# A two-layer graph attention kernel: a front built features first, with spread scores, an adding transfer for the keys and reordered early slots

## What is computed

```python
h = x @ W
e = leaky_relu((h @ a_src)[:, None] + (h @ a_dst)[None, :], 0.2)
valid = (adj > 0) & (h.sum(axis=1) != 0)[None, :]
att = softmax(where(valid, e, NEG)); att = where(valid, att, 0)
L = valid.sum(axis=1)
att = where(att >= 1e-4, att, 0) * L[:, None]      # and 0 where the row's top is not over 1e-4
x = layernorm(x + elu(h + att @ h))
s = leaky_relu(x @ ks.T, 0.2)
x = layernorm(x + softmax(where(adj > 0, s, NEG)) @ ks)
```

## Time and profile before

| | us |
|---|---|
| median of 3 runs | 864.79 |
| lowest, highest | 864.57, 865.67 |
| the profiled execution | 863.84 |
| its span in the trace | 862.0 |

### The profile page before, as it was taken

How to read it: one execution, slowest core, us unless ns; L and a number is a source line. 1 busy time by engine, 2 the same in 40 slices (tenths; PEclk the granted TensorE clock), 3 DMA queues, 4 the chain that set the end, 5 groups by cost and what they waited for, 6 DMA issues and landing times.

```text
span 862.0 us, 17646 instructions
## 1 busy us (share of the span) xinstructions
PE 837.0 (97%) x7111; PEld 718.3 (83%) x7111; DVE 787.5 (91%) x993; ACT 766.2 (89%) x747; POOL 234.1 (27%) x450
## 2 busy tenths in 40 slices
PE   7789999999999999999999999999999999999995
PEld 4668888888988888898888888988888898888885
DVE  2998999999999999999999999999999999999745
ACT  4799999999999999999999999999999999999653
POOL 1371123233212232321223233222232321222100
PEclk9799999999999999999999999999999999999998
DMA  9948766667787666678766666886766678620000
GB/s 221 227 88 164 142 106 121 130 132 137 151 153 107 126 127 130 132 147 154 135 112 122 129 133 139 152 152 103 127 124 136 132 149 154 101 42 21 4 2 10
DMA packets 35713, 105.02 MB, mean 122 GB/s; under 512 B 6960, under 2 KB 19376, under 8 KB 27824
## 3 DMA queue, kind: packets, MB, share of 16 engines
q0 software_dynamic: 16608, 65.02, 51.4%
q1 hardware_dynamic: 18592, 38.80, 12.9%
q10 hardware_dynamic: 432, 0.07, 0.1%
HBM read 136.38 MB, written 2.10 MB: 161 GB/s over the span
## 4 chain that ended last, share of the span: by engine, by line
PE 90%; DVE 3%; POOL 2%; DMA 2%; issue 1%; ACT 1%; POOLq 0%; SPq 0%; ACTq 0%; DVEq 0%
PE bank L342 26%; PE work L243 26%; PE bank L366 13%; PE bank L367 7%; PE work L319 6%; PE work L320 6%; PE work L324 6%; DMA mask<-adj 1%; POOL gate L912 1%; DMA att<-x 1%; PE bank L372 1%; DVE att L729 1%; POOL coef L916 1%; DVE mask L616 0%; ACT att L454 0%
## 5 line engine op out<-in xcount | busy, mean ns | idle before, releaser
L243 PE MATMUL work<-ident,att 128*128 128x128 f32 x2080 | 259.5, 276 | 11.4 <-DMA att<-x 5.7
L243 PEld LDWEIGHTS work<-ident,att 128*128 128x128 f32 x2080 | 236.8, 144 | 19.1 <-issue 6.7
L342 PE MATMUL bank<-h_all,att0T 128*128 128x128 f32 x2048 | 244.3, 275 | 0.0
L342 PEld LDWEIGHTS bank<-h_all,att0T 128*128 128x128 f32 x2048 | 236.2, 192 | 0.2 <-ACT att0T L478 0.2
L366 PE MATMUL bank<-k_parts,att1T 128*128 128x257 f16 x1024 | 182.9, 275 | 0.0
L367 PE MATMUL bank<-k_parts,att1T 128*128 128x129 f16 x1024 | 178.0, 219 | 0.0
L500 ACT ACTIVATE att1T<-work 128x1024 f16<-128x1024 f32 x128 | 131.3, 1027 | 39.2 <-PE work L243 39.2
L695 DVE SCALAR_TENSOR_TENSOR att1T<-work,att1T 128x1024 f16<-128x1024 f32 x128 | 152.2, 1210 | 3.6 <-ACT att1T L500 3.6
L645 DVE SCALAR_TENSOR_TENSOR att<-att,cut 128x2048 f32<-128x2048 f32 x64 | 150.0, 2347 | 0.0
L684 DVE CUSTOM_DVE_ANT_0 att<-att,mask 128x2048 f32<-128x2048 f32 x64 | 146.0, 2284 | 2.4 <-ACT att L484 2.4
L484 ACT ACTIVATE att<-work 128x1024 f32<-128x1024 f32 x128 | 127.7, 1026 | 19.5 <-PE work L324 19.5
(11 more groups left out here) (97 smaller groups left out, 675.4 us busy)
## 6 DMA issues: line engine op xcount, KB each, us to landing
mask<-adj POOLq DMA_DIRECT2D x32, 1024.0 KB, 8.6
mask_zero<-zero_cols SPq DMA_DIRECT2D x29, 1024.0 KB, 5.0
mask_zero<-adj POOLq DMA_DIRECT2D x29, 1024.0 KB, 11.7
att<-x SPq DMA_DIRECT2D x4, 512.0 KB, 6.6
x_sb<-x SPq DMA_DIRECT2D x32, 64.0 KB, 2.8
out<-x SPq DMA_DIRECT2D x32, 64.0 KB, 4.9
k_parts<-ks POOLq DMA_DIRECT2D x1, 1024.0 KB, 12.9
w_sb<-W ACTq DMA_DIRECT2D x1, 64.0 KB, 2.8
```

The lines of the kernel that those rows point to most:

```text
L243: mm = pe.transpose(work[:, n % SLOTS, b * P:(b + 1) * P], source(c * PER + b), ident[:, :])
L342: mm = pe.matmul(acc0, att0T[:, k * P:(k + 1) * P], h_all[:, k, :], start=(k == 0), stop=(k == BLOCKS - 1))
```

## The change

Six things are changed.

1. **Features first, one matrix of 131 columns.** `w_sb` holds W and, beside it, all three columns of W a (source, destination, sum). `make_h` runs right behind the transposes of x, in the fills' order `FIRST`, and gives every block's h and its three numbers, which `keep_parts` puts into `node_parts`. A fourth place (`sums`, two banks) joins the three of `work`. DVE takes chunks 1 and 3 of x and the first two fills of h; ACT takes the rest.
2. **Destination scores and zero columns spread by transposes.** `turn_d` transposes one column of `node_parts`, read 128 times over, so that all rows hold the same 128 scores. `test_zero` (DVE, 8 columns) makes the zero test per node, and `turn_zero` spreads it the same way in bf16, with a bf16 identity. `make_d`, `find_sign`, `zero_quarter` and the widened columns are gone.
3. **Adjacency tile 0 in two halves**, issued when chunks 0 and 2 of x are in; the fp16 keys are issued right behind tile 1 and no longer wait for it, and `k_first` (fp32 keys, SP) waits for tile 1 and no longer for tile 0.
4. **The keys' low parts by an adding transfer.** `negate_k` writes minus the high parts into `k_parts`, and POOL issues a load that adds the fp32 keys to them. `k_parts` is one column wider, so that its rows are of even length. `keep_k_low` is gone.
5. **The first tile.** One exponential over 4096 columns, four cuts of 1024, four separate semaphore counts for the transposes, and the coefficient of tile 0 on DVE.
6. **The first four slots have an order of their own** (`first_slot`, `early_slots` on PE, `early_slot` on ACT and DVE), and slot 3 takes the exponentials of tile 4 and its cut later.

```diff
@@ tensor
+            def make_h(r):
+                blocks = range(r * H_PER, min((r + 1) * H_PER, BLOCKS))
+                c = blocks[-1] // PER
+                pe.wait_ge(w_ready, 1)
+                pe.wait_ge(xT_ready[c % 2], c // 2 + 1)
...
+            def turn_d(c):
+                wait_parts(pe, (c + 1) * PER - 1)
+                turn(place_of("d", c), c, lambda b: node_parts[:, b, 1:2].to_broadcast([P, P])).then_inc(d_turned, 1)
+
+            def turn_zero(k):
+                pe.wait_ge(zero_tested, k + 1)
+                pe.wait_ge(ident16_ready, 1)
+                for b in range(PER):
+                    mm = pe.transpose(zero_place(k)[:, b * P:(b + 1) * P],
+                                      zero_block[:, k * PER + b:k * PER + b + 1].to_broadcast([P, P]), ident16[:, :])
+                mm.then_inc(zero_turned, 1)
...
+            def early_slots():
...
+                sum1(0, 0)
+                turn1(0, 3, True)
+                sum1(0, 1)
+                turn_q(1)
+                sum1(0, 2)
+                for c in range(CHUNKS):
+                    score(1, c)
...
+                sum0(2, 1)
+                sum1(0, 3)
+                turn1(1, 0, True)
+                sum0(2, 2)
+                sum0(2, 3)
@@ vector
-            def keep_k_low():
+            def negate_k():
+
                 dve.wait_ge(k_high, 16)
-                dve.wait_ge(kall_in, 16)
-                nc.vector.tensor_tensor(k_parts[:, :, 0:D], k_first, k_parts[:, :, D:2 * D], ALU.subtract).then_inc(k_low, 1)
+                nc.vector.tensor_scalar(k_parts[:, :, 0:D], k_parts[:, :, D:2 * D], -1.0, None,
+                                        ALU.mult).then_inc(k_negated, 1)
...
+            def test_zero(k):
+                blocks = slice(k * PER, (k + 1) * PER)
+                wait_parts(dve, (k + 1) * PER - 1)
+                nc.vector.tensor_scalar(zero_block[:, blocks], node_parts[:, blocks, 2], 0.0, -NO_EDGE, ALU.is_equal,
+                                        ALU.mult).then_inc(zero_tested, 1)
@@ gpsimd
-            pool.wait_ge(xall_in[1], 16)
-            load_adj(0)
+
+            pool.wait_ge(xall_in[0], 16)
+            nc.gpsimd.dma_start(mask[0][:, half(0)], adj_rows[0][:, half(0)]).then_inc(first_adj_in[0], 16)
+            pool.wait_ge(xall_in[2], 16)
+            nc.gpsimd.dma_start(mask[0][:, half(1)], adj_rows[0][:, half(1)]).then_inc(first_adj_in[1], 16)
             pool.wait_ge(xall_in[3], 16)
             load_adj(1)
 
-            pool.wait_ge(adj_in[1], 16)
             pool.wait_ge(k_one_ready, 1)
             nc.gpsimd.dma_start(k_parts[:, :, D:2 * D], ks.rearrange("(b p) d -> p b d", p=P)).then_inc(k_high, 16)
             load_adj(2)
-            coefficient(0)
-            add_adj(EARLY)
+            add_adj(3)
+            pool.wait_ge(k_negated, 1)
+            nc.gpsimd.dma_start(k_parts[:, :, 0:D], ks.rearrange("(b p) d -> p b d", p=P),
+                                accum_op=ALU.add).then_inc(k_low, 16)
```

More of the change, by code:

```diff
@@ L262, in make_h @@
[L262 to L273 removed]
+                turn(place_of("x", c), c, lambda b: x_all[:, b, :]).then_inc(x_turned, 1)
@@ L386, in first_slot @@
                     score(0, c)
+            def early_slots():
+                score(0, 3)
+                turn0(1, 0)
+                turn0(1, 1)
+                turn0(1, 2)
+                sum0(1, 0)
+                turn0(1, 3)
+                sum0(1, 1)
+                sum0(1, 2)
+                turn1(0, 0, True)
+                turn1(0, 1, True)
+                sum0(1, 3)
+                turn1(0, 2, True)
+                sum1(0, 0)
[5 more added lines that the diff above has]
+                    score(1, c)
+                turn0(2, 0)
+                turn0(2, 1)
+                turn0(2, 2)
+                sum0(2, 0)
+                turn0(2, 3)
+                sum0(2, 1)
[3 more added lines that the diff above has]
+                sum0(2, 3)
+                turn1(1, 1, True)
+                turn1(1, 2, True)
+                turn1(1, 3, True)
+                sum1(1, 0)
+                turn_q(2)
+                sum1(1, 1)
+                for c in range(3):
+                    score(2, c)
             def slot(t):
@@ L422, in _ @@
             first_slot()
-            for t in range(1, TILES):
+            early_slots()
+            for t in range(EARLY_SLOTS + 1, TILES):
                 slot(t)
@@ new lines, in early_slot @@
+            def early_slot(t):
+                u = t - 1
+                copy0(t, 0)
+                copy0(t, 1)
+                raise0(t + 1, t % 2)
+                copy0(t, 2)
+                if t == 1:
+                    copy0(t, 3)
+                raise1(u, 0)
+                raise1(u, 1)
+                if t > 1:
+                    copy0(t, 3)
+                copy1(u, 0)
+                if t > 1:
+                    raise0(t + 1, 1)
+                elu_exp(t)
+                copy1(u, 1)
+                copy1(u, 2)
+                copy1(u, 3)
+                q_high_part(t)
+                bend0(t + 2)
+                for c in range(CHUNKS):
+                    bend1(t, c)
@@ L606, in _ @@
             first_slot()
-            for t in range(1, TILES):
+            for t in range(1, EARLY_SLOTS + 1):
+                early_slot(t)
+            for t in range(EARLY_SLOTS + 1, TILES):
                 slot(t)
@@ L813, in first_slot, with early_slot @@
                 cut(1, 1)
-                zero_mask(3)
+            def early_slot(t):
+                u, w = t - 1, t - 2
+                mask1(u, 0)
+                mask1(u, 1)
+                offset1(u)
+                zero_mask(t + 2)
+                mask0(t + 2)
+                if w >= 0:
+                    finish1(w)
+                low_part1(u, 0)
+                residual0(t)
+                elu(t)
+                low_part1(u, 1)
+                normalise0(t)
+                low_part1(u, 2)
+                threshold0(t + 1)
+                q_low_part(t)
+                low_part1(u, 3)
+                if t + 1 >= EARLY:
+                    build_mask(t + 1)
+                cut(t + 1, 0)
+                cut(t + 1, 1)
             def slot(t):
@@ L828, in slot @@
                     mask0(t + 2)
+                if t == EARLY_SLOTS + 1:
+                    threshold0(t + 1)
+                    cut(t + 1, 0)
                 residual0(t)
@@ L860, in _ @@
             first_slot()
-            for t in range(1, TILES):
+            for t in range(1, EARLY_SLOTS + 1):
+                early_slot(t)
+            zero_mask(EARLY_SLOTS + 3)
+            for t in range(EARLY_SLOTS + 1, TILES):
                 slot(t)
@@ L866, in _ @@
         def _(pool):
-            nc.gpsimd.memset(ones[:, :], 1.0).then_inc(consts_ready, 1)
             nc.gpsimd.memset(ident[:, :], 0.0).then_inc(consts_zeroed, 1)
```

423 lines of the change are left out of this document (239 added, 184 removed).

## The result

| | before | changed |
|---|---|---|
| median of 16 runs each, us | 864.76 | 863.20 |
| lowest, highest | 863.60, 866.10 | 862.65, 863.94 |
| profiled execution, its span | 863.84, 862.0 | 863.02, 861.2 |

The changed kernel is faster by 1.56 us: ratio 0.9984, 95% interval 0.9978 to 0.9990, thus 0.9 to 1.9 us. That is just inside the 0.2% that counts as no change.

What follows compares the result with a forecast made beforehand. The prediction took slot 3's start, set by DVE's list with PE's further lead given back, as the bound: 3.0 us earlier, less 0.6 and 0.2, makes 2.2 us less, 862.6 us. Its range was 859.4 to 866.5.

Steps and rivals of the forecast that it cites:

- it is wrong if slot 3 does not start 3 us earlier on DVE: Its own test: DVE's first layer-1 mask of slot 3 at 114.7 against 117.69, 3.0 us earlier.
- the sum 3.0 - 0.6 - 0.2: DVE's earlier slot 3, less the threshold wait in slot 3, less the collision with POOL's load: 2.2 us gained.
- no slot becomes shorter: Slots 3 to 31: left as they are apart from small edits in slot 3, still 24.9 us each.
- PE's start: Front: small loads in at 6.6 us, half pace to 10.4, then h fills and x chunks at full pace to 16.3.
- The late rise of the clock: Rival, PE in the front: clock stays at its lower level throughout, ledger 12 us later, 876.8; chance 0.03.
- slow transposes: Rival, PE's fills from 16.3 to 25.4: broadcast transposes take double, -1.0 to -6.2 us, 867.5 in one case; chance 0.09.
- slow negation: Rival, DVE in the first slot: negation takes 4.4 us instead of 1.2, total -0.8, 865.6; chance 0.08.
- late tile 1: Rival, DVE's mask in the front: adjacency tile 1 lands at 23, not about 20.8, total -1.0, 865.8; chance 0.12.
- The collision with POOL's adding load of tile 3: Near 40.3 us its issue meets DVE's mask of tile 2: full price 0.9, or nothing; 0.2 taken.
- The adding key load: POOL in the first slot: issue of some 1.72 us after the negation, x1 of tile 0 at 55.9, transfer hidden.
- PE's lead is given back: Early slots: PE 5.4 us earlier, DVE only 3.0; slot 3 gives back the 2.4 between them.
- The 0.6 us for the threshold in slot 3: Slot 3: threshold of tile 4 waits 0.6 us for an exponential that ACT now does later.

Runs made afterwards that it cites:

- e3: Changed kernel with POOL issuing the adding key load behind the deviation of tile 0, not ahead of it: 860.02 us, ratio 0.9947 to the kernel before.
- e4: Changed kernel with the order of slots 1 to 3 on PE, ACT and DVE put back to the old one: 862.99 us, ratio 0.9980.
- e9: e3 with the order of slots 1 to 3 on PE, ACT and DVE put back to the old one: 859.12 us, ratio 0.9946.
- e1: Kernel before with only the rows of k_parts made 258 columns long, not 257: 863.93 us, ratio 0.9990.
- e2: Changed kernel with the rows of k_parts back at 257 columns: 864.19 us, ratio 0.9998 to the kernel before.
- e6: e3 with PE's first work reordered, x chunk 0 turned ahead of the weights and the wait for the small loads: 858.59 us, ratio 0.9943.
- e10: Changed kernel with 35 identity transposes that compute nothing in PE's wait ahead of x1 of tile 0: 861.78 us, ratio 0.9968.
- e11: e6 with 13 identity transposes that compute nothing in PE's gap ahead of x1 of tile 0: 859.23 us, ratio 0.9936.
- e12: e7 with 13 identity transposes in PE's gap ahead of x1 of tile 0 and 18 at the very start: 856.88 us, ratio 0.9908.
- e7: e6 with DVE building the mask of adjacency tile 1 one step later: 859.73 us, ratio 0.9944.
- e8: Changed kernel with the keys' low parts made by DVE's subtraction again and no adding load: 864.19 us, ratio 1.0002 to the kernel before.

## Why the prediction was right, and where it was not

The forecast was 862.6 and the measurement 863.2, but not by the forecast's own sum: it said itself that it is wrong if slot 3 does not start 3 us earlier on DVE, and it started 0.04 earlier. The time came out near by luck: of the sum 3.0 - 0.6 - 0.2 nothing was there in the profiles, and a term that the sum did not have, the even rows, made about half to two thirds of the gain.

**What bounds the kernel.** Right in the main: DVE's list, with what it waits for in it, decides when slot 3 begins (e3, e4, e9). Wrong in one sentence, that no slot becomes shorter. The padding column stood in the change's description as a matter of even rows, and was priced at nothing. It gave 0.72 us in the traces, 0.85 by e1's median and 1.0 by e2's.

**PE's start.** The first step that failed. The small loads: taken 6.6, measured 7.26. Then the first h fill was counted at full pace from 10.4; it began at 11.24 and took 2.11 to the next start, not 1.38. Together 1.6 us, and the cuts start 1.8 later than forecast (37.78 against 36.0). The late rise of the clock was a rival at 3 in 100, but only in the form that it never rises in the front. That it may rise one fill later was in no case.

**Spread by transposes, copies, negation.** All as forecast: 1.04 for eight fp32 broadcast transposes, 1.23 for a copy of 1024, 1.22 for the negation. The rivals on slow transposes, slow negation and late tile 1 all fell; DVE's mask of tile 1 did not wait. It would have with a front 1.1 us faster (e6). That rival's price does not add up: 2.0 us late and 1.8 for the test are 3.8, where 3.4 was taken. The collision with POOL's adding load of tile 3, put at 0.2, cost DVE nothing: its mask of tile 2 took 1.22 from 42.56 on, beside an issue of 1.25 us from 42.92. In e3 the issue started first (41.30, against 41.65 for the mask), and there both were longer, 1.93 and 1.47.

**The adding key load.** The second step that failed. Its place in POOL's list was seen, its size was not: 1.72 was taken from the plain load of the same shape, and it is 3.20, thus 1.5 us. With the 1.8 us of the front and some 0.4 of small steps, x1 of tile 0 came at 59.60, not 55.9: 3.7 late. Its transfer was hidden, as forecast: it landed 16.6 us after issue, and the first key sum began at 80.94 without a wait.

**First scores.** They "ran slowly before and do so again": true, and taken as given. It was a price of some 1.4 us (58.05 against 56.64 from x1 to slot 3) with a cause, PE's wait ahead of x1, and e10 removes it. The longest wait of PE, 11.86 us ahead of the first attention transposes, also left them slow (24 in 4.97 us, where 2.78 is full pace), but DVE's residual at 53.76 did not wait for PE: not every such gap is on the chain.

**Early slots.** PE in chunk 3 of tile 2 at 113.88 against 110.8, DVE at 117.65 against 114.7: both 3 us late, of the 3.7 that they inherited. The difference between the two, 3.8 us, was forecast as 3.9. So the ledger was sound there, and its conclusion that PE's lead is given back too. The 0.6 us for the threshold in slot 3 came (0.56), but in the place of two waits of 0.31 and 0.28 that slot 3 had before: that term was zero.

**What stays open.** The medians are 1.56 us apart, and the even rows explain 0.7 to 1.0 of it. The rest, 0.6 to 0.8, is not in the two profiles, where slot 3 starts at the same time. The profile before lies 0.9 us under its median, that of the changed kernel 0.2 under its own. In e1, with the front of the kernel before, x1 of tile 0 was 0.19 later than in that profile and slot 3 1.01 later, at a granted clock of 0.66 and not 0.83. So the rest may well be the clock behind x1, lower in more of the executions before than after; one profile each can't show it. Nor is it shown what makes the two groups in the runs of e6 and e11.

## What to carry to other kernels

Count the waits of TensorE by what they do to the work behind them too: after waits of 1.75 to 4.45 us on this kernel's critical chain, products at half pace cost 1.3 to 2.9 us more. Cheap filler transposes in such a gap gave 0.16% (e10 against the changed kernel), and together with some before the first load lands 0.36% (e12 against e7); the whole change had given 0.16%. When profiles differ by a us, compare them from one mark on, and at the same granted clock. Behind a small result that everybody waits for, put the transfer's issue, not ahead of it, and price an adding transfer by itself. And look at the steady loop's operands even when a change is said to touch only the front: a row length multiplies by every slot.

## What was not expected of the hardware

- Products that read 257 and 129 fp16 columns from rows of 514 bytes cost more than from rows of 516: 0.025 us in each slot of 64 products (24.898 and 24.899 us in the two traces with odd rows, 24.872 or 24.873 in the other twelve).
- Issuing an adding load (fp32 to fp16, 128 x 32 x 128) took 3.20 to 3.24 us on POOL, wherever it stood; the plain one 1.71 to 1.72.
- TensorE fell to 1.2 GHz after a wait of 1.75 us in one run (e3), and kept 2.4 GHz after waits of 1.50 in three (e6, e7, e9). The wait of 2.98 us in the last slot differs likewise between runs: behind it 24 transposes took 2.99 us in e1, e3, e6, e7, e11 and e12, while 32 took 6.54 in e8 and 6.66 in e10.
- Transposes of the identity alone brought TensorE to 2.4 GHz (e12: eight in 1.09 us behind eighteen in 3.58), and kept it there through a gap (e10: granted clock 1.00 and not 0.70).
- A transpose whose operand is one column read 128 times costs as much as any other: 1.04 us for eight.
